# A reordered opening in a fused attention and mixture-of-experts kernel

## The reference

```
x = x + tanh(g_xattn) * CrossAttention(LayerNorm(x), ctx)          # 16 heads of 16, biases on q, k, v, o
h = LayerNorm(x) * ln_g + ln_b
logits = h @ Wr                                                    # 7 routed experts
top 2 experts a token, softmax over the two, capacity 732 slots an expert, first come first served
routed = sum over the two of gate * (silu(xe @ W1) * (xe @ W3)) @ W2
shared = (silu(h @ W1s) * (h @ W3s)) @ W2s                         # 256 -> 1024 -> 256, all tokens
x = x + tanh(g_ffn) * (routed + shared)
```

## Time and profile before

| | us |
|---|---|
| median of 3 runs | 878.38 |
| lowest, highest of them | 878.12, 883.29 |
| the profiled execution's own time | 886.02 |
| span of the profiled execution | 883.8 |
| mean granted TensorE clock in it | 0.971 of 2.4 GHz |

### The profile page before, as it was taken

How to read it: one execution, slowest core, us unless ns; L and a number is a source line. 1 busy time by engine, 2 the same in 40 slices (tenths; PEclk the granted TensorE clock), 3 DMA queues, 4 the chain that set the end, 5 groups by cost and what they waited for, 6 DMA issues and landing times.

```text
span 883.8 us, 14663 instructions
## 1 busy us (share of the span) xinstructions
PE 839.1 (95%) x5262; PEld 729.9 (83%) x5262; DVE 590.3 (67%) x1292; ACT 387.7 (44%) x717; POOL 320.2 (36%) x243
## 2 busy tenths in 40 slices
PE   8788999999999999999999999999999999999991
PEld 7465685886858868688688899999999999999990
DVE  4565768878778787888877576565656657565340
ACT  5425426345363263533725445353544445453330
POOL 4830303033012150031224603818375472814333
PEclk9788799999999999999999999999999999999996
DMA  6632041311412214112130722334434332431111
GB/s 227 163 72 64 11 120 36 98 35 39 119 37 66 65 38 119 36 39 62 33 120 11 215 84 80 65 106 95 114 83 86 101 79 69 101 65 20 17 19 19
DMA packets 93984, 66.93 MB, mean 76 GB/s; under 512 B 55110, under 2 KB 80892, under 8 KB 93928
## 3 DMA queue, kind: packets, MB, share of 16 engines
q1 hardware_dynamic: 40312, 55.40, 22.1%
q0 software_dynamic: 53088, 10.30, 8.5%
q10 hardware_dynamic: 528, 0.52, 0.2%
HBM read 37.38 MB, written 14.27 MB: 58 GB/s over the span
## 4 chain that ended last, share of the span: by engine, by line
PE 81%; issue 3%; ACT 3%; DVE 3%; POOL 1%; DMA 0%; DVEq 0%; ACTq 0%; POOLq 0%
PE bank L1608 21%; PE bank L1610 21%; PE bank L1609 21%; PE bank L1840 3%; PE bank L1841 2%; PE bank L1842 2%; PE bank L1732 2%; PE bank L1726 2%; DVE row_max L1278 2%; PE bank L1696 2%; ACT float_data L1100 1%; ACT probabilities L1100 1%; PE bank L1882 1%; PE bank L1794 1%; PE bank L1803 1%
## 5 line engine op out<-in xcount | busy, mean ns | idle before, releaser
L1608 PE MATMUL bank<-split_operands 128*128 128x366 f32 (+4 forms) x1148 | 383.6, 334 | 4.0 <-POOL split_operands L919 2.3
L1609 PE MATMUL bank<-split_operands 128*128 128x366 f32 (+4 forms) x1148 | 377.8, 329 | 0.0
L1610 PE MATMUL bank<-split_operands 128*128 128x366 f32 (+4 forms) x1148 | 377.6, 329 | 0.0
L1608 PEld LDWEIGHTS bank<-split_operands 128*128 128x128 f32 (+1 forms) x1148 | 215.6, 188 | 24.3 <-issue 9.0
L1610 PEld LDWEIGHTS bank<-split_operands 128*128 128x128 f32 (+1 forms) x1148 | 215.4, 188 | 12.3
L1609 PEld LDWEIGHTS bank<-split_operands 128*128 128x128 f32 (+1 forms) x1148 | 215.8, 188 | 9.6
L1018 POOL DMA_INDIRECT out<-float_data,scatter_now x42 | 125.7, 2994 | 185.6 <-DVE float_data L1571 108.7
L1591 DVE TENSOR_TENSOR hidden<-bank,float_data 128x366 f32<-128x366 f32 x112 | 60.4, 540 | 114.1 <-PE bank L1610 114.1
L1197 ACT ACTIVATE float_data<-bank 128x366 f32<-128x366 f32 x112 | 53.5, 477 | 113.7 <-PE bank L1610 113.7
L1194 ACT CAST split_operands<-hidden 128x366 fp32r<-128x366 f32 x112 | 55.7, 497 | 68.4 <-DVE hidden L1591 68.4
L993 POOL DMA_INDIRECT float_data<-z_scratch,gather_now x42 | 72.8, 1733 | 17.4 <-issue 16.2
(11 more groups left out here) (156 smaller groups left out, 1062.9 us busy)
## 6 DMA issues: line engine op xcount, KB each, us to landing
float_data<-in_L_ffn_W SPq DMA_DIRECT2D x21, 1024.0 KB, 8.7
split_operands<-split_operands SPq DMA_DIRECT2D x96, 128.0 KB, 2.3
float_data<-in_x SPq DMA_DIRECT2D x8, 512.0 KB, 4.3
z_scratch<-float_data SPq DMA_DIRECT2D x8, 512.0 KB, 3.1
out<-float_data SPq DMA_DIRECT2D x7, 512.0 KB, 2.9
split_operands<-split_operands SPq DMA_DIRECT2D x8, 192.0 KB, 3.8
float_data<-in_L_ffn_W1s SPq DMA_DIRECT2D x2, 512.0 KB, 9.8
float_data<-in_L_ffn_W3s SPq DMA_DIRECT2D x2, 512.0 KB, 8.0
```

The source lines that it names most:

```text
L1608: pe.matmul(o, lhs[0], rhs[0], start=first, stop=False)
L1609: pe.matmul(o, lhs[0], rhs[1], start=False, stop=False)
L1610: return pe.matmul(o, lhs[1], rhs[0], start=False, stop=last)
```

## The change

The two lists are rewritten, and the steps are fitted to them:

- Block 0's tokens are loaded first, and its norm comes ahead of the keys' products. Block 1's statistics are taken before block 0's queries leave their banks.
- `kbd` is no longer built by transfers. GpSimd multiplies the keys with a mask of 8 columns (`own_head`) in `spread_keys`.
- For block 0 ScalarE issues the eight transfers of the queries' high halves (`stack_hi`) and SP only the four of the low halves.
- `queries` uses `hi_first`: what needs only the high part of the tokens runs first. In block 0 the same is done in `project_first` and in `first_up`.
- The first maxima wait for the queries' high part alone, and the values' products stand in three groups between the maxima.
- Scores of block 0 run without the queries of block 1 between them. The splitting of the shared expert's weights is spread otherwise (6 pieces low before the first scores' end, 4 after the attention, 2 after the second norm), with waits that hold GpSimd until VectorE has done its norms.
- Block 1's last maxima move behind the first `up`, and three `up` instead of two stand ahead of block 1's scores. Later in the second period `maxima` and `up` and `down` change places, and the first of the next block's maxima transposes stands ahead of the eighth `up`.
- The number of `keep_busy` matmuls changes from 18+4+4+4+4+8+18+12 to 18+4+8+15.

```diff
 def first_period(do, b):
     n = b.next()
     do("keep_busy", 2, 18, "ident_ready", 1)
+    do("stats_x", b)
+    do("rest_const")
     do("context")
+    do("scale_x", b)
     do("weights", 1)
+    do("weights", 0)
+    do("transpose_x", b)
     do("project_keys")
-    do("keep_busy", 2, 4, "ident_ready", 1)
-    do("stats_x", b)
-    do("weights", 0)
-    do("scale_x", b)
     do("bias_keys")
-    do("transpose_x", b)
+    do("spread_keys")
     do("weights", 2)
-    do("keep_busy", 2, 4, "ident_ready", 1)
+    do("stats_x", n)
     do("queries", b)
     do("keep_busy", 3, 4, "ident_ready", 1)
     do("queries_out", b)
+    do("residual", b)
     do("keys", b)
-    do("residual", b)
+    do("stack_hi", b)
     do("stack", b)
-    do("shared_weights")
-    for t in range(TT):
-        do("maxima", b, t)
-        if t == 1:
-            do("keep_busy", 6, 4, "xl_ready", KD)
-        if t == 2:
-            do("project_values")
+    do("shared_hi", 0, 2)
+    do("maxima", b, 0)
+    do("maxima", b, 1)
+    do("project_values", 0, 1)
+    do("maxima", b, 2)
+    do("project_values", 1, 2)
+    do("maxima", b, 3)
+    do("project_values", 2, B)
     do("maxima_T", b)
-    do("keep_busy", 4, 8, "m_done", TT)
     do("stack_maxima", b)
+    do("shared_hi", 2, 3)
+    do("scale_x", n)
+    do("shared_lo", 0, 1)
+    do("values_out")
+    do("shared_lo", 1, 6)
+    do("transpose_x", n)
     do("more_shared")
-    do("values_out")
-    norm(do, n)
+    do("keep_busy", 2, 8, "m_done", TT)
     do("first_scores", b)
-    do("transpose_x", n)
     do("route_const")
     do("scores", b, 0)
-    do("shared_hi", 3, 5)
-    do("shared_lo", 6, 10)
+    do("scores", b, 1)
     do("queries", n)
-    do("scores", b, 1)
+    do("attention_hi", b)
+    do("project", b)
     do("queries_out", n)
     do("stack", n)
+    do("shared_hi", 3, 6)
+    do("shared_lo", 6, 10)
+    do("project_out", b)
     do("maxima", n, 0)
+    do("keep_busy", 2, 15, "m_done", TT)
+    do("norm2", b)
     do("maxima", n, 1)
-    do("attention_hi", b)
-    do("project", b)
-    do("shared_hi", 5, 6)
+    do("transpose_z", b)
     do("shared_lo", 10, NPIECE)
-    do("project_out", b)
+    do("residual", n)
     do("maxima", n, 2)
-    do("keep_busy", 3, 18, "m_done", TT + 2)
-    do("norm2", b)
-    do("transpose_z", b)
-    do("maxima", n, 3)
-    do("keep_busy", 2, 12, "m_done", TT + 3)
...
 def second_period(do, b):
     up(0)
+    do("maxima", b, 3)
+    up(1)
     do("maxima_T", b)
     do("stack_maxima", b)
-    up(1)
-    do("hidden", f, 1)
+    up(2)
     do("logits", f)
+    do("first_scores", b)
     do("logits_T", f)
-    do("first_scores", b)
     nxt("stats_x")
+    nxt("scale_x")
+    do("hidden", f, 2)
     nxt("keys")
     do("scores", b, 0)
-    nxt("scale_x")
-    nxt("residual")
     do("scores", b, 1)
-    up(2)
+    up(3)
     do("attention_hi", b)
     nxt("transpose_x")
-    up(3)
     do("project", b)
+    nxt("residual")
     do("project_out", b)
...
     do("pick", b, 0)
+    nxt("maxima", 1)
     up(6)
-    nxt("maxima", 1)
+    nxt("maxima", 2)
     down(4)
-    nxt("maxima", 2)
-    down(5)
     nxt("maxima", 3)
     do("pick", b, 1)
-    up(7)
+    down(5)
     nxt("maxima_T")
     nxt("stack_maxima")
+    up(7)
     down(6)
...
+        def spread_keys():
+            pool.wait_ge(sig["heads_ready"], 1)
+            for k in range(KD):
+                pool.wait_ge(sig["k_hi"], k + 1)
+                pool.tensor_tensor(kbd[:, k], k_s[:, 0, k, 0:SK].bitcast(F32).unsqueeze(1).broadcast_to([P, 8, SK]),
+                                   own_head[:, :].unsqueeze(2).broadcast_to([P, 8, SK]), ALU.mult)\
+                    .then_inc(sig["kbd_spread"], 1)
...
         def split_shared(first, last):
+            if first == 0:
+                pool.wait_ge(sig["xn_ready"], 2 * TT)
+            if first == 10:
+                pool.wait_ge(sig["z_ready"], TT)
...
         def attention_lo(b, half):
+            if b.at(0):
+                pool.wait_ge(sig["attn_done"], NG)
...
+        def stack_hi(b):
             act.activation(tgx[:, :], gx, ACT.Tanh).then_inc(sig["tanh_done"], 1)
             act.activation(tgf[:, :], gy, ACT.Tanh).then_inc(sig["tanh_done"], 1)
-            for h in range(3):
-                split_shared(h)
+            act.wait_ge(sig["qh_ready"], KD)
+            for r in range(4):
+                for base in (0, 64):
+                    act.dma_start(qst[base:base + 32, r::4, :].bitcast(F32), q_of(b)[32 * r:32 * r + 32, 0].bitcast(F32)).then_inc(sig["qst_loaded"], 16)
...
+        def hi_first(o, lhs, rhs, low):
+            for k in range(KD):
+                pe.matmul(o, lhs[k][0], rhs[k][0], start=(k == 0), stop=False)
+                pe.matmul(o, lhs[k][1], rhs[k][0], start=False, stop=False)
+            if low:
+                pe.wait_ge(*low)
+            for k in range(KD):
+                mm = pe.matmul(o, lhs[k][0], rhs[k][1], start=False, stop=(k == KD - 1))
+            return mm
...
         def maxima(b, t):
             if b.at(0):
                 if t == 0:
                     pe.wait_ge(sig["k_lo"], KD)
+                    pe.wait_ge(sig["qh_ready"], KD)
+                    pe.wait_ge(sig["kbd_spread"], KD)
+                elif t == 1:
                     pe.wait_ge(sig["ql_ready"], KD)
-                    pe.wait_ge(sig["kbd_loaded"], 128)
-                elif t >= 2:
+                else:
                     pe.wait_ge(sig["m_done"], t - 1)
             elif b.at(1):
-                pe.wait_ge(sig["m_done"], TT + max(t - 1, 0))
+                pe.wait_ge(sig["m_done"], TT + t)
...
+        def first_up(b):
+            pe.wait_ge(sig["wsplit_lo"], 3 * NSTEP0)
+            pe.wait_ge(sig["hh_ready"], KD)
+            for w in range(2):
+                for k in range(KD):
+                    for j in range(2):
+                        pe.matmul(bank[w][:, :], W0[:, j, w, k * FF:k * FF + P], hTs[0][:, 0, k], start=(k + j == 0), stop=False)
+            pe.wait_ge(sig["hl_ready"], KD)
+            for w, ready in ((0, sig["a_ready"]), (1, sig["b_ready"])):
+                for k in range(KD):
+                    mm = pe.matmul(bank[w][:, :], W0[:, 0, w, k * FF:k * FF + P], hTs[0][:, 1, k], start=False, stop=(k == KD - 1))
+                mm.then_inc(ready, 1)
```

162 lines of the change are left out of this document (93 added, 69 removed).

## The result

| | before | after |
|---|---|---|
| median of 11 runs each | 878.54 (877.03 to 885.28) | 873.46 (869.11 to 876.26) |
| ratio of the times, 95% interval | | 0.9913 (0.9886 to 0.9939) |
| profiled execution: time / span / clock | 886.02 / 883.8 / 0.971 | 873.46 / 871.7 / 0.974 |

The kernel became faster by 0.9%, where 1.8% was forecast (863.0, range 854 to 873). The profiled execution itself went from 886.0 to 873.5, by 12.6, where the sum said 15.4; the medians differ by 5.1 only. Both gaps have to be explained, and they turn out to have different causes.

The account below looks back on a forecast made before the run. TensorE was taken to bound the kernel, with slack only in the opening. Terms of -17.0 plus 1.6 for semaphore gaps gave -15.4, so 886.0 profiled became 870.6; carrying over 7.6 to the unprofiled median gave 863.0, range 854 to 873.

Parts of the forecast that it names:

- block 0's attention at half clock too: Rival: block 0's attention also runs at half clock, +5.2 us, giving 868.2; chance 0.28.
- (1) Tokens first: Block 0's first scores: statistics no longer wait for key weights; -1.9 us, bounds 0 and -3.8.
- (2) Maxima and mask products: Block 0's first maxima need only the queries' high part, -0.9 us; GpSimd's mask products taken as 0, bounds 0 and +1.5.
- (3) The values in pieces: Block 0's fourth maximum: VectorE no longer waits behind all values' products, which come in pieces; -1.1 us.
- (4) and (5), the second queue: Block 0's stack: SP no longer delays the copied maxima, -1.7 us; ScalarE issuing eight high halves adds 0.3.
- The first up's waits: Block 0's last value products to first up: 4.8 and 9.8 us, 0.3 for lateness, 1.7 for a clock dip.
- The hold on GpSimd: After block 0's attention, GpSimd waits for VectorE's norm: +0.5 us; L1300 kept undisturbed, counted as nothing, at most -1.
- The third up: Ahead of block 1's first scores: adds 2.8 us there, no help in the wait for table load and exponentials.
- The tail: Before block 2's first scores: ups cover the waits on reductions and the stack's transfer; -1.9 us.
- The same 745 us behind these: Behind block 2's first scores: the rest has no slack, stays 745 us, and gives none of the gain back.
- Late links: Rival: GpSimd or ScalarE misses its slots in the opening; with half clock +10 us in all, 873; chance 0.15.
- full clock throughout: Rival: block 1's attention also holds 2.4 GHz, -5.5 us more, giving 857.5; chance 0.15.

Follow-up runs that it names:

- after_again: The kernel after run once more, nothing edited; profiled execution 870.55 us, median 875.17, ratio 0.9923 to the kernel before.
- before_look3: The kernel before, nothing edited, third further look for a trace of its quicker group; 875.99 us.
- fill_both: The kernel after with 12, 10 and 18 more identity products in the waits around block 0's and behind block 1's first scores; 868.65 us, ratio 0.9851.
- before_again: The kernel before once more, nothing edited; block 2's first scores at 134.1; its span and that of another unedited repeat were 880.0 and 880.2 us.
- one_queue: fill_both with SP issuing the eight high halves of block 0's stack too, ScalarE none; 871.65 us, ratio 0.9906.
- trimmed: fill_both without the hold on GpSimd and with 13, 4 and 8 identity products instead of 20, 10 and 18; 866.12 us, ratio 0.9813.
- fill_first: The kernel after with 12 more identity products ahead of block 0's first scores and 10 behind them; 871.72 us, ratio 0.9882.
- tokens_third: fill_both with block 0's tokens loaded third, behind context and key weights; 873.29 us, ratio 0.9928.
- no_hold: fill_both without the wait that holds GpSimd's low part of block 0's attention until VectorE finishes the norms; 868.44 us, ratio 0.9866.

## Why the prediction failed by what it did

**The sum came out right, in part by luck.** Where the clocks were as forecast (first attention 2.4 GHz, second 1.2) there is an execution to hold it against, the one called after_again: first scores 28.4 (forecast 27.9), last value products 38.9 (38.1), first up 54.1 (54.7), exponentials 68.0 (68.6), block 2's first scores 121.8 (123.1), span 868.5 (883.8 less 15.4 is 868.4). Its time was 870.55, forecast 870.6. That it meets within 0.1 is luck. Block 2's first scores came 16.7 us sooner and not 15.4: the allowance of 1.6 for small semaphore gaps was hardly needed there (17.0 were summed without it), and 1.4 were given back behind them, where I saw no slack. Several terms, further down, miss by as much.

**The step that failed** is the last: "the unprofiled median 878.38 stands 7.6 below it, and the difference carried over gives 863.0". Of the 10.5 us between 863.0 and the measured 873.46, these 7.6 are the carrying over: the median run of after is its profiled execution itself, and nothing stands between them. The other 2.9 are the clock of the first attention: I took full clock there for the likeliest, and this execution had half clock in it; the one with full clock took 870.55.

A part of the 7.6 was clock, too. The profiled execution of before had both at 1.2 GHz and belonged to the slower group of its kernel's runs; I computed against it a kernel that wins 5.2 by a full clock in the first attention, and then took off the 7.6 as well. What the quicker runs of before have over their slower ones was, as far as the traces tell, partly counted twice, and partly was not to be had in the new order: before_look3 shows block 1's attention at 1.00, worth 5.4 us, and no dip ahead of it, worth 0.9, while the kernel after lacks the first in both traces and has no such dip to lose.

From like to like the change gives 12.1 by span with both attentions at half clock (883.8 to 871.7), 11.5 with the first back at full (880.0 to 868.5), and 6.8 with both at full (873.8 in before_look3 to 867.0 in fill_both). Between the midmost runs of the quicker groups it is 8.4 (878.1 to 869.7), of the slower ones 8.8 (883.7 to 874.9): some 3 less than the first two, which fits with before's groups holding clock patterns that after's don't, but isn't shown. From median to median it is 5.1: another 3 less, because the median of before lies in its quicker group (7 of 11) and that of after is the quickest run of its slower one (6 of 11). None of these times is dear for being profiled: unprofiled runs of before took up to 886.7. Which attention has which clock in the runs of 877 to 879, the median of before among them, wasn't traced (mean clock 0.982 to 0.985): the traced executions took 876 and 882 to 886. What the 7.6 are made of stays open to that extent.

**The rival that named the profiled run** was block 0's attention at half clock too. It gave 868.2 by the same carrying over, which is 875.8 for the profiled execution; measured 873.5. Its milestones held: last value products 43.3, measured 43.4. I gave it 0.28. Which of the two patterns a run takes isn't settled by the program alone. I had weighed it by a page. The Trainium skill, TensorE: Matmul & The Clock Gate, Part 4: PE-mode transpose, says that transposes don't count as TensorE being busy in the same way. The runs neither bear this out nor refute it: the same transposes stood ahead of an attention at 1.00 and of one at 0.50, and with 22 identity products more it was at 1.00 in every trace.

**Why the second attention of after fell.** The forecast of a fall there was right in both its traces. TensorE stands 1.75 us in one piece ahead of block 1's second pair of scores (1.74 in the other trace), and filling of that wait alone kept the clock. In the kernel before the third up's place was elsewhere and the wait came in two pieces, 1.07 us ahead of the logits' transposes and 0.93 behind the first scores in before_look3. before_again has the same two pieces (1.06 and 0.91) and fell. So there too one program went both ways, and why it sometimes held is not shown.

**Term by term:**

- *(1) Tokens first*, taken as -1.9 with -3.8 as bound: with the tokens third the new order loses 4.6, of which 3.2 are the norm and 1.4 a fall of the clock. The bound held for the first; the clock was left out. In the change itself the first maximum came 3.5 sooner (15.98 against 19.50), where (1) and (2) said 2.8.
- *(2) Maxima and mask products*: 2.41 for the two on GpSimd against an estimated 3.0, done 1.2 before the maximum. First maximum 15.98, where 19.50 less 1.9 and 0.9 is 16.7.
- *(3) The values in pieces*, -1.1: from first maximum to the copy of the maxima it took 9.1 before and 7.9 after, -1.3.
- *(4) and (5), the second queue*: -1.7 and +0.3 were wrong as a saving. The copy was done at 29.18 and sent at 30.88 before; after, it was done at 24.40 and sent at 26.07. SP is at its low halves in between both times, since they start at 23.35 only, behind six transfers of the keys on the same queue (18.49 to 23.31). From copy to first scores it is 4.6 in both kernels, and the 1.4 never came; the 4.8 that the first scores gained are (1) to (3), summed as 3.9. What the second queue does is to keep the rest: taken away from the new order it costs 2.3 at the first scores and 3.0 in time. The Trainium skill's rule that issuing engines are not separate DMA queues (DMA: Bandwidth & Descriptors) would, as I had worked it out, have left 1 us less still. The rows of one_queue show the issue time itself, 9.6 us for fourteen, ahead of the maxima, and saving issue time is the part that the rule grants. ScalarE's 0.66 an issue ends the rival of a blocked ScalarE.
- *The first up's waits*: 14.9 from last value products to the first up and 1.7 for a dip of the clock; measured 15.2 in both traces of after, at 1.00 but for the end of the first attention's half clock (0.68 at 44 to 46) in the profiled one. The dip never came, and 54.7 was met within 0.6 only because the end of the attention was 0.8 late. GpSimd's power began 0.5 behind VectorE's statistics, within the bound.
- *The hold on GpSimd*, +0.5 and at most -1 for L1300: +0.4 at the projection, 0.2 in time, within the scatter. With it off, L1323 (L1300 before) keeps its 0.42 there, by a start 0.03 us ahead of GpSimd.
- *The third up* "is no help in the wait": this was wrong in its reading. It covers not the exponentials' wait but the transfer of the stacked maxima ahead of the first scores, which I had not thought of; moved back it costs 3.5.
- *The tail*, -1.9: 1.3 at first scores, 1.5 in time.
- *"The same 745 us behind these"*: 746.8, so 1.5 us are given back. The timeline of the kernel after shows where the first of it goes:

```profile
125.02 1.28 ACT L1121 ACT_TABLE_LOAD   x1
...
135.92 0.50 PE L1631 MATMUL bank<-split_operands 128*128 128x512 f32 x1
```

Block 2's scores are sooner, but ScalarE is at the table load at 125.02 and the first up behind comes 11.0 after them (10.6 in the earlier trace rows). That is 0.4 of the 1.5; the other 1.1 is spread over the 735.8 us that remain (734.7 before), and I found no single place for it.

**Late links and full clock throughout**: no queue missed a slot, and none of the 21 runs of the kernel after reached the clock 0.990 that both attentions at 2.4 GHz show. fill_both has that pattern: 867.0 by span, where the rival's sum gives 862.9. It pays 1.0 at the first scores for products that outlast the wait, and 2.2 between block 1's first and second scores; trimmed, with 25 products against 48, is at 864.8.

## What to carry to other kernels

A hand schedule is made against one execution, and can be no better than the step that takes it to the median: before carrying a difference over, find out which clocks the profiled run had and which the median's runs have, by profiling the same kernel several times. Where runs of one kernel fall into groups with different granted clocks, compare like with like, and fill the wait that decides with just as many idle products as it holds. An up put ahead of a wait should be asked for every wait that it then stands in front of, not for the one that it was meant for.

## What the runs showed of the hardware

- The same program had TensorE at 2.4 GHz in one execution and at 1.2 in another in the same 10 us, with first scores at 28.37 and 28.44, and waits of 1.20 and 1.41 us ahead of them; the difference was 4.5 us and stayed to the end but for 1.3.
- A single wait of 1.75 us ahead of scores that then alternate with ScalarE came with half clock in all three traces that have it (after, after_again, fill_first); with 18 identity products in it, or 8, neither was there. In the kernel before, the same two waits of 1.1 and 0.9 us were followed by 1.00 in before_look3 and by 0.50 in before_again.
- In tokens_third a wait of 3.21 us on the normed tokens was followed by half clock at 14 to 16, 1.4 us of time.
- A DMA issue for the stack cost 0.73 us on SP in one_queue, 0.66 on ScalarE.
- Where VectorE's 128x256 norm and GpSimd's 128x512 low part met, the one that started first kept its time and the other was stretched: 0.42 and 1.55 us with VectorE 0.03 ahead (no_hold, 40.55), 1.54 and 1.28 with GpSimd 0.02 ahead (the kernel before, 432.23).
